# Sixteen more identity multiplications on TensorE in the landmark block, and its five tables of order written anew

## The reference, cut to what matters

```python
kernel1 = softmax(q @ k_lm.T)          # 512 tokens x 64 landmarks, per head
kernel2 = softmax(q_lm @ k_lm.T)       # 64 x 64, per head
kernel3 = softmax(q_lm @ k.T)          # 64 x 512, per head
# iterative_inv(kernel2), six times:
KV = K @ V
V = 0.25 * V @ (13*I - KV @ (15*I - KV @ (7*I - KV)))
SV = kernel1 @ V @ (kernel3 @ v)
out = SV @ w_proj
```

## Time and profile before

| | us |
|---|---|
| median of 3 runs | 1116.17 |
| lowest and highest of the 3 | 1111.09, 1122.37 |
| the profiled execution | 1124.09 |
| its span, first to last instruction | 1121.9 |
| TensorE busy in the span | 933.2 (83%) |
| mean granted clock of TensorE, as a share of 2.4 GHz | 0.925 |

### The profile page before, as it was taken

One profiled execution on the slowest core, in us unless ns is written; L12 is line 12 of the kernel. 1 busy time (PEld: TensorE's weight loads), 2 busy tenths in 40 slices (PEclk: granted clock), 3 DMA queues, 4 the chain that ended last, 5 costly groups with the idle time before them and its releaser, 6 DMA issues. The chain is left out here.

```text
span 1121.9 us, 37263 instructions
## 1 busy us (share of the span) xinstructions
PE 933.2 (83%) x15213; PEld 666.9 (59%) x15213; DVE 831.1 (74%) x2089; ACT 641.6 (57%) x1387; POOL 472.3 (42%) x443
## 2 busy tenths in 40 slices
PE   7899989998989888677888986597689989772898
PEld 5567667675766665456566665454466666552653
DVE  3899899888557996567776687878487898685556
ACT  2456656782664574456667585356376776382630
POOL 2355345227356630445524156512543454446421
PEclk8899989999999999888999998689789999895999
DMA  9700000002321100120101101100311110102533
GB/s 319 254 3 3 4 2 3 3 3 95 115 72 58 31 8 13 38 68 12 49 21 52 41 12 35 30 29 2 102 42 50 39 46 20 49 26 90 160 105 99
DMA packets 51079, 61.71 MB, mean 55 GB/s; under 512 B 5601, under 2 KB 46177, under 8 KB 50913
## 3 DMA queue, kind: packets, MB, share of 16 engines
q1 hardware_dynamic: 43584, 42.51, 11.8%
q0 software_dynamic: 5760, 15.74, 4.4%
q10 hardware_dynamic: 1568, 1.09, 0.3%
HBM read 29.70 MB, written 29.62 MB: 53 GB/s over the span
## 5 line engine op out<-in xcount | busy, mean ns | idle before, releaser
L764 POOL TENSOR_TENSOR a_pr<-a_pr,a_smax 128x512 f32<-128x512 f32 x128 | 133.3, 1042 | 177.5 <-DVE a_smax L877 168.0
L1267 POOL TENSOR_TENSOR b_tm<-b_aw,b_sq 128x640 f32<-128x640 f32 (+1 forms) x48 | 65.4, 1362 | 148.9 <-ACT b_sq L1505 143.5
L871 DVE TENSOR_TENSOR a_pr<-a_bank,a_mask 128x512 f32<-128x512 f32 x128 | 82.8, 682 | 42.0 <-PE a_bank L1066 34.7
L963 ACT ACTIVATE a_pr<-a_pr 128x512 f32<-128x512 f32 x128 | 78.6, 630 | 51.9 <-POOL a_pr L764 44.1
L1247 POOL TENSOR_TENSOR b_pa<-b_pa,b_amax 128x512 f32<-128x512 f32 x64 | 67.1, 1048 | 70.3 <-ACT b_pa L1470 61.8
L969 ACT ACTIVATE a_pT<-a_bank 128x512 f32<-128x512 f32 x128 | 71.1, 596 | 41.2 <-PE a_bank L1075 30.0
L1075 PE MATMUL a_bank<-ident,a_pr 128*128 128x128 f32 x512 | 76.4, 289 | 20.2 <-ACT a_pr L963 17.6
L1256 POOL TENSOR_TENSOR b_pa<-b_pa,b_asum 128x512 f32<-128x512 f32 x64 | 66.7, 1043 | 58.4 <-DVE b_asum L1371 54.2
L307 POOL DMA_INDIRECT rows_sorted<-f_rows,f_pos x60 | 58.2, 969 | 72.2 <-DVE f_pos L403 53.8
L1398 DVE SCALAR_TENSOR_TENSOR b_aw<-b_tm,b_inverse 128x320 f32<-128x320 f32 (+1 forms) x144 | 63.4, 440 | 33.1 <-PE b_inverse L1646 13.7
L318 POOL DMA_INDIRECT f_rows<-results_sorted,f_pos x60 | 58.6, 977 | 66.9 <-issue 34.4
(11 more groups left out here) (238 smaller groups left out, 2359.8 us busy)
## 6 DMA issues: line engine op xcount, KB each, us to landing
f_xg<-rows_sorted SPq DMA_DIRECT2D x42, 256.0 KB, 3.2
results_sorted<-f_yg SPq DMA_DIRECT2D x42, 256.0 KB, 2.3
rows_sorted<-f_yg SPq DMA_DIRECT2D x2, 2944.0 KB, 18.5
X<-in_x SPq DMA_DIRECT2D x7, 512.0 KB, 11.0
out<-X SPq DMA_DIRECT2D x7, 512.0 KB
experts_w<-in_e_wT SPq DMA_DIRECT2D x2, 1024.0 KB, 9.3
rows_sorted<-f_rows,f_pos POOLq DMA_INDIRECT x60
f_rows<-results_sorted,f_pos POOLq DMA_INDIRECT x60
```

Of the source, the lines that this page charges most:

```text
L764: nc.gpsimd.tensor_tensor(out=pr[:, u % AHEAD], in0=pr[:, u % AHEAD], in1=smax[:, u % AHEAD, :].unsqueeze(2).broadcast_to([P, HQ, KEYS]), ...
L871: pre.emptied(V_.tensor_tensor(out=pr[:, u % AHEAD], in0=gb[:].rearrange("p (h k) -> p h k", h=HQ), in1=mask[:, u // 4, :].unsqueeze(1).br ...
L963: nc.scalar.activation(pr[:, u % AHEAD], pr[:, u % AHEAD], ACT.Exp, scale=float(HD) ** -0.5)\
L1267: nc.gpsimd.tensor_tensor(out=tm[:, a:b, k], in0=aw3[:, a:b, k], in1=sq[:, a:b, k], op=ALU.subtract).then_inc(s_tm, 1)
```

## The change

Each of the eight batches gets two items more, `idle2` and `idle3`, placed by the table; these new ones have two products, the old ones keep three. So TensorE has 28 such items with 68 products in the block, where it had 12 with 36. A new item takes its place in the ring like any other, so the banks of all items behind it move on by one.

```diff
@@ -1524,7 +1524,8 @@
                 if item.startswith("idle"):
 
                     ring.filled(mm(gb[:, 0:P], ident[:], ident[:], start=True, stop=True), n, item)
-                    mm(gb[:, 0:P], ident[:], ident[:], start=True, stop=True)
+                    if item in ("idle0", "idle1"):
+                        mm(gb[:, 0:P], ident[:], ident[:], start=True, stop=True)
                     ring.emptied(mm(gb[:, 0:P], ident[:], ident[:], start=True, stop=True), n, item)
                     return
                 if item[:2] == "xT":
```

All five strings of `LANDMARK_ORDER` are replaced. They hold the same items as before but for the sixteen; only where each stands differs. The start of TensorE's string, and the lines around the end of batch 3:

```diff
@@ -1848,161 +1849,162 @@
 
 LANDMARK_ORDER = {
     "pe": """
-        0.idle0 0.xT0 0.xT1 0.q0 0.k0 m1.rx3.0 0.q1 m1.rx3.1 0.k1 0.v0 0.v1 0.S20 0.S21 0.S22 m1.lg3 0.S23 0.idle1
...
-        3.R4.0 3.N4.0 3.R5.0 3.ta3 3.ta4 3.ta5 2.pj2 3.ta6 3.N5.0 3.ta7 3.idle1 2.pj3 3.Z 3.sv0 3.sv1 3.pj0 3.pj1
-        3.pj2 4.xT0 3.pj3 4.xT1 4.q0 4.k0 4.q1 4.k1 m2.rx0.0 m2.rx0.1 m2.lg0 4.sc0 4.v0 4.tc0 4.v1 m2.lt0 m2.rx1.0
...
+        3.ta7 2.pj2 2.pj3 3.N5.0 4.xT0 4.xT1 3.Z 4.q0 3.sv0 3.sv1 4.k0 3.pj0 3.pj1 3.pj2 3.pj3 4.q1 4.k1 4.v0 4.v1
...
+        4.idle3 m2.rx0.0 m2.rx0.1 4.S20 4.sc0 m2.lg0 5.idle2 m2.rx1.0 m2.rx1.1 4.tc0 4.tc1 m2.lg1 m2.lt0 4.S21 4.w0
```

298 lines of the change are left out of this document (150 added, 148 removed).

## The result

| | before | changed |
|---|---|---|
| median of the runs, us | 1118.73 (4 runs, 1111.09 to 1122.37) | 1141.67 (4 runs, 1138.27 to 1145.87) |
| profiled execution's span, us | 1121.9 | 1136.5 |

The changed kernel takes 1.0216 times as long, with a 95% interval of 1.0148 to 1.0284: 23 us more by the medians, 24 by the ratio. The forecast was 1109 with a range of 1094 to 1127, so it has the wrong sign and the result lies outside its range.

The account below looks back on a forecast made before the run. TensorE, busy 83% of the span, was taken to pace the kernel, though not as a wall, its clock falling at waits. Terms 3.5 - 2.5 - 3 - 2 - 3 = -7.0 took the median 1116.17 to 1109 us, range 1094 to 1127.

Parts of the forecast that it names:

- a, the items: Sixteen new items on TensorE: ten in dense stretches cost 4.4 us, partly covered, no ring waits taken; +3.5 us.
- b, the clock: Dense stretches, four short windows of low clock: identity products fill gaps and win back a third of 7.6; -2.5 us.
- The rival of the held clock: Dense stretches and batch 3: added products hold TensorE's clock at full speed, term b the full -7.6; 1093 us, chance 0.12.
- c, the opening: 455 to 500 us: batch 1's work fills a third of TensorE's 9.7 us of waits; -3 us; sign: 0.R0.0 no later.
- d, the end of batch 3: Batch 4's products fill waits ahead of 3.Z to 4.q0, gain 10; gathers and co0, co1 cost 8; -2 us.
- e, batch 4's first iteration: GpSimd's step of 4.R0.0, moved behind the sixth scatter, starts earlier and saves TensorE waits of 2.23 and 0.78; -3 us.
- The rest: From 962 us to the end: tables nearly alike, m3's scatter ahead of the tail as before; 0 us.
- The gathers in the chain: Slower rival: VectorE and GpSimd wait in batch 3's iterations for m1's rows, d +14; 1134 us, chance 0.13.
- one said that they could win there: Rival: new order alone cuts idle time in 500 to 685 and 812 to 962 by a fourth; about 1099 us, chance 0.10.
- only the cost: Rival: orders only move waits, the clock falls as often, the sixteen items cost 3.5; 1120 us, chance 0.25.

Follow-up runs that it names:

- x2: Kernel before in its old orders, with only the sixteen new items added; 1.0054 of the kernel before, 6 us.
- x15: x1 with the old orders from 645 to 693 us of the kernel before; 1.0130 of the kernel before.
- x17: x1 with the old orders from 505 to 575 us of the kernel before; 1.0250 of the kernel before.
- x8: Kernel before with the new orders, without new items, for the end of batch 3 alone (693 to 742 us); 1.0023 of the kernel before.
- x3: Changed kernel with m1.ga0 to m1.ga7 and m1.co0 to m1.co4 back at their old places in batch 3's chain; 1.0210 of the kernel before.
- x6: x1 with the old orders on all engines from 630 to 693 us of the kernel before; 1.0170 of the kernel before.
- x14: x1 with the old orders from 630 to 655 us of the kernel before alone; 1.0256 of the kernel before.
- x10: x1 with m1.bi0 and VectorE's four additions of it moved later, m1.bi0 to behind 3.w5; 1.0199 of the kernel before.
- x16: x1 with m1.bi1 behind 2.Z, its additions, m1.co0 and m1.co1 behind 3.U0.0, GpSimd's 3.R0.0 ahead of three gathers and 3.na2; 1.0286 of the kernel before.
- x18: x1 with ScalarE's copy 3.D0.0 moved directly behind 3.R0.0, ahead of 2.sv0 and 2.sv1; 1.0194 of the kernel before.
- x19: x1 with the moves of x18 and x10, plus m1.bi1's additions, VectorE's 2.N5.0 and 3.R0.0, first four gathers, co0 and co1 moved; 1.0207 of the kernel before.
- x13: The same kernel as x1, run again as a base; 1.0169 of the kernel before.
- x1: Changed kernel's five new orders without the sixteen new items; 1.0156 of the kernel before.
- x7: x1 with the old orders for the opening of batch 4 (742 to 796 us of the kernel before); 1.0306 of the kernel before.

## Why the prediction was wrong

**a, the items: +3.5.** The mechanism and the size were near. x2 gives 6 us (3 to 9), and the changed kernel stands 0.5 to 0.6% above its orders alone. The 7 us of products were a good guide; that I took no ring waits was not, since the largest loss of x2 is at one place where two unread banks stand ahead of an item that takes four. The rule of the ring that the text leaned on (a wait only where another engine lags) is right: in that place VectorE did.

**b, the clock: -2.5.** Of the four windows, at the same times, two went to 1.00, one stayed at 0.89 and the last fell to 0.58. Moved with the work, as the prediction asked, they are at 1.00, 1.00, 0.90 and 1.00 (the last at 835.9 to 844.3), but what fell only moved: 300 to 324 as a whole has 0.74 for 0.73 before, new stretches fell, and the mean is 0.923 for 0.925. Zero. The rival of the held clock, with the rule of the Trainium skill behind it ("TensorE: Matmul & The Clock Gate", What's actually happening: activity releases the throttle), did not come in by adding products; but x15 agrees with the rule the other way round: in the same work the clock was 1.00 where the engines did not wait for each other and 0.79 to 0.82 where they did.

**c, the opening: -3.** Work 0 to 60 takes 77.5 us for 79.3 and 78.5, so -1 to -2, made of -3 in 24 to 60. Its sign failed: 0.R0.0 starts at 482.72, 9.5 us later than before (473.23), and only 0.N0.0 is earlier, 492.18 for 494.58. And the next 60 us of work take 5 us more (73.4 for 69.0 and 67.8). x17 brings back 3 of them.

**d, the end of batch 3: -2.** This is the step that failed. Its gain was there (228 to 252 is 8 to 9 us shorter, 10 were expected), and it did not last: I had asked what the products ahead of 3.sv0 fill, and not what is late next. x8 shows that all of it is waited for in the opening of batch 4, with any order there; the changed kernel loses more than that, 12.4 us in 252 to 276. Its price was put on the gathers and `m1.co0`. VectorE never waited for them (691.13, no gap), and with them back in place nothing changes (x3). That TensorE and ScalarE come to a stop while three gathers are issued (3.69 us of ScalarE) had a likeness in the rows of before at the scatters, 0.78 us inside a group of TensorE; I used it there and didn't carry it here.

**What d left out** is the loss itself: the 12 to 14 us between `3.sa0` and `3.R1.0`. The text costed the places at which the table visibly moved something (co and gathers ahead of 3.R0.0) and counted the dense stretches, in which "all orders are written anew", as zero change unless they got better. How much is written anew can be counted: of the 213 items that TensorE starts between 500 and 685 in the kernel before only 106 keep their order among each other. x15 and x6 show that the orders of this one stretch of 48 us cost 12 to 15 in the quicker sets, x14 that those just before cost nothing, x10, x16, x18 and x19 that none of the items moved there does, alone or together.

What in the sequence does it is argued, not shown. Between R and N of a batch stand the steps of three other engines (3.2 us from 2.R5.0 to 2.N5.0 in the old table), in which TensorE needs other work, but not more than fits. In the old string the items between 2.R3.0, N3, R4, N4, R5, N5, 3.R0.0 and 3.N0.0 are 6, 2, 6, 3, 2, 1 and 3; in the new one 5, 1, 1, 2, 3, 6 and 5. Missing fillers are not what costs: five of six are gone between R4 and N4, and R4 to R5 is shorter than before (6.7 us for 8.2). Longer are the places with more items: R5 to N5 (5.7 for 3.2), N5 to 3.R0.0 with six items for one (5.0 for 1.8), and 3.R0.0 to 3.N0.0 (9.9 for 3.8 in x13). So the likeliest reading is that other work stands ahead of chain steps that could start, as x19 shows at 3.N0.0 (5.9 us late) and at 3.R0.0 (2.92). R3 to R4 (10.2 for 7.4), with fewer items, does not fit it. To move 2.sv0, 2.sv1, 3.ta0 and 3.ta1 behind 3.N0.0, and 3.tc6 to 3.w7 ahead of 2.R5.0, would test it.

**e, batch 4's first iteration: -3.** The size came out, the reading of the rows did not. GpSimd's step begins at 810.34 without a gap (816.82 and 8.73 us before), and work 300 to 324 takes 39.7 us for 43.6, 42.2: 3 us. But the row of before names ScalarE's copy (L1505) as what the step waited for, and the last scatter had ended at 808.08: the step was not held by the scatters ahead of it, but by TensorE's 4.R0.0, which took from 799.71 to 811.22. And the 2.23 us at 825.71 are ahead of 4.N1.0, a wait for VectorE, not for this step. In x8, the old tables there in a quicker set, 4.R0.0 is not drawn out and the same work takes 33.4 us; x14, x15 and x17 with the new ones take 38.8 to 39.5. So the gain of 3 is luck of the slower sets; in the quicker ones these orders lose about 6 here.

**The rest: 0.** "The tables are nearly alike" was too strong: of the 143 items that TensorE starts after 962 in the kernel before, 104 keep their order among each other. 324 to 492 takes 8 us more (210.9 for 202.5 and 201.4) and 492 to the end 4 less. Where it is lost varies between executions of one table (456 to 480: 37.6 and 34.6 us in x1 and x13), and in the quicker sets little of that loss is there (31 to 33 us in x6, x7, x14 to x17, 29 to 30 in the kernel before). I leave it open; in 456 to 480 of the changed kernel a clock of 0.77 for 0.94 goes with it.

**The chances.** "The gathers in the chain" had 0.13 and came nearest with its time, 1134, for the wrong reason. No case said that orders written anew could lose in the dense stretches, though one said that they could win there; with 28.6 us of idle time in one of them the loss was as open as the gain, and the case for it belonged beside the other with at least the same chance. A quarter of that idle time more instead of less (10.7 us on top of the 1120 of "only the cost") would have been 1131, still short of 1141.67.

## What to carry to other kernels

When the order of a whole program is rewritten, count between each two steps of its longest chain how many items of other work stand there now and stood there before, over all of it, not only at the ends and at the transfers; a chain that keeps its place in the work lost ten microseconds and more here, most likely by what had come to stand ahead of its steps. A gain at one place counts only up to the next wait: ask what the work moved ahead would have hidden there. And an item that takes a place in a ring costs most just ahead of one that takes several.

## What the runs showed of the hardware that was not expected

The same kernel, the same order, and two clocks: in x1_orders_only and x13_orders_again (identical programs) the work from 264 to 276 ran as

```profile
766.40:787.50 21.10, 14.85 (x252) 11.41 (x249) 16.49 (x43) 17.55 (x42) 3.08 (x4) 0.81 0.04 12
```

```profile
767.20:792.70 25.50, 20.54 (x249) 15.60 (x250) 16.75 (x43) 17.64 (x42) 3.11 (x4) 0.55 0.03 9
```

with 14.85 and 20.54 us of busy time and a clock of 0.81 and 0.55; the second, though it had the fewer gaps, took 4.4 us more. Both have the same wait of TensorE near the start, 2.18 us for VectorE; behind it the clock was back within some 4 us in the one and stayed low in the other. So the clock's fall behind one wait can cost more than the wait, and differently in each execution.

Between sets the kernel before differed by 3 to 4% (medians of 1081 and 1085 us in two sets, 1116 to 1124 in the others). The chip by its number is not what sets it: chip 11 ran both a set with 1118 and the one with 1085. Most stand where GpSimd issues indirect DMAs one behind the other. In the changed kernel three gathers in 3.6 us cut the 32 products of 2.Z into five pieces and hold ScalarE back for 3.69 us. In x14_mid_early_old, with the same items and the same three gathers (678.48 to 682.00) in a quicker set, nothing of it is seen:

```profile
679.14 1.09 PE L1655 MATMUL b_bank<-b_aw,b_k2n 64*64 64x16 f32 x32
```

```profile
679.41 0.89 ACT L1498 ACTIVATE b_sq<-b_inverse 64x320 f32<-64x320 f32 x2 [1.13 <-PE b_inverse L1634]
```

At the scatter of m2 in the kernel before five products of 4.R0.0 start 1.4 us apart from 801.55 on; in x8_end3_new, with the same orders there and the same sixteen scatters, 4.R0.0 is one piece of 0.78 us. So it is not the indirect DMAs alone that stop the other engines. What does it in some sets and not in others is open.

It also bears on the ratios. Those of kernels with the new orders almost whole were larger in the quicker sets (x7, x14, x16, x17: 1.025 to 1.031) than in the slower ones (x1, x13: 1.016, 1.017). The kernel before has twice as much of these waits as the changed one, so in a slower set it loses more by them, and part of what the new orders cost is hidden; that this is the whole of the difference is not shown. The loss of the stretch between `3.sa0` and `3.R1.0` is not one of these stops: x14 has it in full without them.
